# Moving the statistics of the third token tile behind the second tile's k projection

## The chip, the cores and the metric

The kernel runs on all 8 cores of one Trainium2 chip (two dies, cores 0 to 3 and 4 to 7). The same program runs on every core, with other data; the cores exchange nothing. The time is the device time of the slowest core, in microseconds (us).

## What is computed

A layer norm of x (4 x 4096 x 1024), then an attention-like branch and a feed-forward branch with ternary weights, both added to x:

```python
xn = _layernorm(x)
# attention branch
qkv = einsum('btd,de->bte', xn, Wqkv) + bqkv
q, k, v = split(qkv, 3)
q = q / norm(q);  k = k / norm(k)
kv = sum(k * v, axis=-2, keepdims=True)      # over all 4096 tokens of a batch
attn = einsum('btd,de->bte', q * kv, Wout) + bout
# feed-forward branch (tlin = matmul with ternary w, scaled by s)
h = silu(tlin(xn, w1)) * tlin(xn, w2)
h = gelu(tlin(h, h1));  h = gelu(tlin(h, h2))
out = x + attn + tlin(h, w3)
```

The sum kv runs over all tokens of a batch entry. Each core writes 2048 tokens, but computes k and v for all 4096 tokens of its batch entry.

## The kernel before

The data lie feature-major: 128 features on the partitions, tokens along the free axis. Tokens are taken in tiles of TT = 1024. Tiles g = 0 to 3 cover all 4096 tokens for k and v; tiles 4 and 5 are tiles 0 and 1 again, now for q and the feed-forward branch. The big buffer Gb has three regions for normalised tiles; tiles 0, 1 and 2 lie in regions 0, 1 and 2 (REGION), tile 3 in region 0 again.

A small scheduler (class Sched) records each operation with its engine and the tokens it waits for, and emits them engine by engine in the order in which they were recorded. So the order of the Python calls is the order in each engine's queue. SP's queue issues x loads, POOL's (GpSimd) weight loads, and PE, DVE and ACT have one queue each. S.emit() ends a block of the program; there are two blocks, and the engines meet between them.

The pieces that matter:

- plan_stats(g) (L202): for each of 8 feature chunks an x load of 512 KB into one of two slots xs (L185), a cast to bf16 on DVE (L210), a Square on ACT (L214), and four matmuls with a matrix of ones, which sum x into PSUM tile PA and x squared into PB. Then a tail on DVE and ACT (L237 to L251) makes the reciprocal deviation rstd_b and u_b. Then the 8 chunks of x are loaded a second time and normalised into Gb with two DVE operations each (L259 and L261). These eight are called xn(g) below.
- plan_proj: 4 weight units (512 KB each, ring of 5 slots) of two output chunks each. An output chunk is 16 matmuls of 128x512, which need all 8 normalised chunks, into one of the PSUM tiles PC, PD, PB in turn. An evacuation on ACT frees the PSUM tile: L393 for k, L312 for q, L416 for v. For k and q a Square (L398, L317) and two matmuls with ones into PA follow for each chunk.
- plan_norm_rstd (L297, L301): Ln and Exp on ACT of the norm in PA, written to rstdn_b. The Ln waits for the last norm matmul and, by extra=[st["kv_prev_dve"]], for the plan_kv before it, which still reads rstdn_b.
- plan_kv: for 8 chunks two large DVE operations (L366, L369) and a tiny addition to kv_acc (L373). Below it is kv(0) for t = 0 and kv(1) for t = 1.

All of it that matters here is the first block. Its order is: stats(0) with xn(0); for t = 0: k projection of tile 0, its norm, stats(1) with xn(1), v projection of tile 0, stats(2) with xn(2), kv(0); for t = 1: k projection of tile 1, its norm, q projection of tile 4, v projection of tile 1, kv(1). In the prediction k(0), v(0), k(1), q and v(1) are these projections. The second block begins with stats(3) and the first feed-forward projections; tile 2 is read only after them, in the segment loop that makes k and v of tiles 2 and 3.

Of the kernel before, what the change touches and what calls it, by code (L numbers as in the profile page):

```python
# [106 lines left out]
def build_program(stop=None):  # L107
# [16 lines left out]
    with ExitStack() as _ctx:  # L124
# [26 lines left out]
        PA = en(nc.psum_tensor("PA", [128, TT], F32))  # L151
        PB = en(nc.psum_tensor("PB", [128, TT], F32))
# [36 lines left out]
        def dma_w(unit_ap):  # L189
            j, slot, ftok = w_ring.next()  # L190
            tok = S.op("gpsimd", lambda e, o=slot, i=unit_ap: e.dma_start(out=o[:, :], in_=i),  # L191
                       waits=[ftok], inc=w_ring.semn[j])
            return j, slot, tok

        def mm(ps_name, hs, lhsT, rhs, start, stop, waits=(), inc=None):
            return S.op("tensor",
                        lambda e, p=PS[ps_name], h=hs, l=lhsT, r=rhs, a=start, b=stop:
                        e.matmul(p[:, h * 512:(h + 1) * 512], l, r, start=a, stop=b),  # L198
                        waits=waits, inc=inc)
# [72 lines left out]
        def plan_proj(units, g, evac, ping=("PC", "PD", "PB"), pre=None):  # L272
            xn_toks = xn_toks_g[g]
            k = 0
            for iu, (unit_ap, ocs) in enumerate(units):
                jw, wslot, tw = pre[iu] if pre is not None else dma_w(unit_ap)
                last_tok = None
                for jo, oc in enumerate(ocs):
                    ps = ping[k % len(ping)]
                    k += 1  # L280
                    t_mm = None
                    for kc in range(DC):
                        for hh in range(2):
                            t_mm = mm(ps, hh,
                                      wslot[:, kc * 256 + jo * 128: kc * 256 + (jo + 1) * 128],
                                      xn_sl(g, kc, hh),
                                      start=(kc == 0), stop=(kc == DC - 1),
                                      waits=[tw, psum_free[ps], xn_toks[kc]],
                                      inc="s_pe" if (kc == DC - 1 and hh == 1) else None)
                    last_tok = t_mm  # L290
                    psum_free[ps] = evac(oc, ps, t_mm)
                w_ring.set_free(jw, last_tok)

        def plan_norm_rstd(norm_ps, norm_last, dst=None, extra=()):
            if dst is None:
                dst = rstdn_b
            t_ln = S.op("scalar", lambda e, p=norm_ps, d=dst: e.activation(  # L297
                d[:, :], PS[p][:, :], AF.Ln),
                waits=[norm_last] + list(extra), inc="s_ac")
            psum_free[norm_ps] = t_ln  # L300
            t_rk = S.op("scalar", lambda e, d=dst: e.activation(  # L301
                d[:, :], d[:, :], AF.Exp, scale=f32(-0.5)),
                waits=[t_ln], inc="s_ac")
            return t_rk
# [53 lines left out]
        with (  # L358
            nc.sbuf_tensor("kB2", [128, DC * TT], BF16) as kB2,
            nc.sbuf_tensor("vA", [128, DC * TT], BF16) as vA,  # L360
            nc.sbuf_tensor("vB", [128, DC * TT], BF16) as vB,
            nc.sbuf_tensor("prod", [128, TT], F32) as prod,
        ):
            def plan_kv(kbuf, vbuf, t_rk, kev, vev):
                for oc in range(DC):
                    tp = S.op("vector", lambda e, o=oc, kb=kbuf, vb=vbuf: e.tensor_mul(  # L366
                        prod[:, :], kb[:, o * TT:(o + 1) * TT], vb[:, o * TT:(o + 1) * TT]),
                        waits=[kev[oc], vev[oc]], inc="s_dv")
                    tm = S.op("vector", lambda e, o=oc: e.scalar_tensor_tensor(  # L369
                        prod[:, :], prod[:, :], 1.0, rstdn_b[:, :], ALU.mult, ALU.mult,  # L370
                        accum_out=kvp[:, o:o + 1]),
                        waits=[tp, t_rk], inc="s_dv")
                    st["kv_done"] = S.op("vector", lambda e, o=oc: e.tensor_add(  # L373
                        kv_acc[:, o:o + 1], kv_acc[:, o:o + 1], kvp[:, o:o + 1]),
                        waits=[tm], inc="s_dv")
                st["kv_prev_dve"] = st["kv_done"]
                if kbuf is qkvt:
                    st["kv_dve_par0"] = st["kv_done"]

            plan_stats(0, "PA", "PB")  # L380
            xn_toks_g[4] = xn_toks_g[0]
            for t in range(NT1):
                kbuf = qkvt if t % 2 == 0 else kB2
                vbuf = vA if t % 2 == 0 else vB
                kev, vev = {}, {}
                norm_last = [None]

                pend_n = []

                def k_evac(oc, ps, t_mm, _kb=kbuf, _kev=kev, _nl=norm_last):  # L390
                    if len(pend_n) >= 2:
                        pend_n.pop(0)()
                    tk = S.op("scalar", lambda e, o=oc, p=ps: e.activation(  # L393
                        _kb[:, o * TT:(o + 1) * TT], PS[p][:, :], AF.Identity,
                        bias=cst[:, 8 + o:9 + o]),
                        waits=[t_mm], inc="s_ac")
                    jq, qslot, fq = sq_ring.next()
                    tq = S.op("scalar", lambda e, o=oc, q=qslot: e.activation(  # L398
                        q[:, :], _kb[:, o * TT:(o + 1) * TT], AF.Square),
                        waits=[tk, fq], inc="s_ac")  # L400

                    def nmm(oc_=oc, jq_=jq, qslot_=qslot, tq_=tq):
                        t_n = None
                        for hh in range(2):
                            t_n = mm("PA", hh, ones_sb[:, :], qslot_[:, hh * 512:(hh + 1) * 512],
                                     start=(oc_ == 0), stop=(oc_ == DC - 1),
                                     waits=[tq_, psum_free["PA"]],
                                     inc="s_pe" if hh == 1 else None)
                        sq_ring.set_free(jq_, t_n)
                        _nl[0] = t_n  # L410
                    pend_n.append(nmm)
                    _kev[oc] = tk
                    return tk

                def v_evac(oc, ps, t_mm, _vb=vbuf, _vev=vev):
                    tv = S.op("scalar", lambda e, o=oc, p=ps: e.activation(  # L416
                        _vb[:, o * TT:(o + 1) * TT], PS[p][:, :], AF.Identity,
                        bias=cst[:, 16 + o:17 + o]),
                        waits=[t_mm], inc="s_ac")
                    _vev[oc] = tv  # L420
                    return tv

                plan_proj([(wqkv[4 + i, :, :], [2 * i, 2 * i + 1]) for i in range(4)],
                          t, k_evac, pre=st.get("pre_k"))
                while pend_n:
                    pend_n.pop(0)()
                t_rk = plan_norm_rstd("PA", norm_last[0],
                                      extra=[st["kv_prev_dve"]])
                if t == 0:
                    plan_stats(1, "PA", "PB")  # L430
                if t == NT1 - 1:
                    plan_qproj(4)
                plan_proj([(wqkv[8 + i, :, :], [2 * i, 2 * i + 1]) for i in range(4)],
                          t, v_evac)
                war[t % 3] = S.pe_tok()
                st["pre_k"] = ([dma_w(wqkv[4 + i, :, :], ) for i in range(4)]
                               if t + 1 < NT1 else None)
                if t == NT1 - 1:
                    st["pre_ffn"] = [dma_w(w1[0, :, :]), dma_w(w2[0, :, :])]
                if t == 0:  # L440
                    plan_stats(2, "PA", "PB")
                plan_kv(kbuf, vbuf, t_rk, kev, vev)

            if stop == "p1":
                S.op("sync", None, waits=[st["kv_done"]])
            S.emit()
# [336 lines left out]
```

How the kernel before makes its waits and increments, by code:

```python
            def body(eng):  # L69
                for _, fn, waits, tok in items:
                    for wt in waits:
                        sname, val = wt[0], wt[1]
                        key = (ename, sname)
                        if self.done.get(key, 0) >= val:
                            continue
                        eng.wait_ge(self.sems[sname], val)
                        self.done[key] = val
                    if fn is not None:
                        inst = fn(eng)
                        if tok is not None:
                            inst.then_inc(self.sems[tok[0]],
                                          16 if tok[0] in self.DMA_SEMS else 1)
```

## Time and profile before

| | us |
|---|---|
| median of the 2 runs shown | 3077.19 |
| lowest, highest | 3072.51, 3081.87 |
| profiled execution, device time | 3087.21 |
| its span (slowest core, core 2) | 3085.7 |
| PE busy in the span | 2882.0 (93%) |
| DVE busy, ACT busy | 378.6 (12%), 464.6 (15%) |

The profile is one execution; times are us from the start of a core's span unless marked ns. A row of the timeline gives the start, the length, the engine, the line, the operation with what it writes and reads and its shape, the count of instructions merged, and in brackets how long the engine was idle before it and what ended that. Lengths of merged matmul groups are modelled and may overlap the next group by a fraction of a us; the distance between starts is the safer measure.

### The profile page before, as it was taken

How to read it: one execution, taken by the hardware profiler on the slowest of the kernel's cores; microseconds unless marked ns; L12 is line 12 of the kernel's file. 1: busy time of each engine (PE TensorE's matmuls, PEld its weight loads, DVE VectorE, ACT ScalarE, POOL GpSimd, SP SyncE). 2: the span in 40 equal slices, each digit the busy share in tenths (PEclk: the TensorE clock that was granted, in tenths of full speed). 3: DMA queues.
4: the chain of work that ended last, by engine and by line, in shares of the span. 5: the costliest groups of instructions: out<-in, count | busy, mean ns of one | idle time of the engine just before them, and what ended most of it. 6: DMA issues, size and time to landing. Idle time of an engine off the chain costs nothing.

```text
span 3085.7 us, 30706 instructions; the slowest of 8 cores (3046.7 to 3085.7 us)
## 1 busy us (share of the span) xinstructions
PE 2882.0 (93%) x13056; PEld 1283.0 (42%) x13056; DVE 378.6 (12%) x440; ACT 464.6 (15%) x463; POOL 219.9 (7%) x420
## 2 busy tenths in 40 slices
PE   3876799899999999999988899999999999999987
PEld 0322244344444444444433344444444444444433
DVE  3254211443000000000011221100000000000011
ACT  1433211351000000000020031100000000000100
POOL 0000000010000000000000000000000000000000
PEclk8888799999999999999999999999999999999998
DMA  6561544785444444444445654444444444444453
GB/s 162 126 159 32 116 80 72 156 137 96 76 77 78 78 75 76 75 78 78 77 102 116 130 97 75 82 74 77 75 75 76 77 78 78 75 75 76 75 107 92
DMA packets 76598, 278.93 MB, mean 90 GB/s; under 512 B 8752, under 2 KB 8880, under 8 KB 76464
## 3 DMA queue, kind: packets, MB, share of 16 engines
q0 software_dynamic: 59904, 218.13, 42.6%
q1 hardware_dynamic: 16560, 58.85, 6.4%
q8 instruction: 105, 1.72, 0.2%
q14 instruction: 29, 0.24, 0.0%
HBM read 486.66 MB, written 8.39 MB: 160 GB/s over the span
## 4 chain that ended last, share of the span: by engine, by line
PE 82%; DMA 5%; DVE 2%; ACT 1%; issue 0%; SPq 0%; DVEq 0%; ACTq 0%
PE PD L198 23%; PE PC L198 23%; PE PB L198 18%; PE PA L198 18%; DMA xs<-x_fm 3%; DMA out_fm<-os 1%; DVE os L701 1%; DVE os L695 0%; ACT os L667 0%; DVE xb L210 0%; DVE tmp_f L259 0%; ACT Ab L626 0%; DVE Ab L498 0%; DVE Gb L261 0%; DVE rstd_b L242 0%
## 5 line engine op out<-in xcount | busy, mean ns | idle before, releaser
L198 PE MATMUL PC<-Gb,wr 128*128 128x512 bf16 x2080 | 479.0, 383 | 23.1 <-DVE Gb L261 23.1
L198 PE MATMUL PD<-Gb,wr 128*128 128x512 bf16 x2080 | 474.3, 381 | 0.0
L198 PE MATMUL PB<-Gb,wr 128*128 128x512 bf16 x1728 | 393.0, 381 | 4.1 <-DVE rstd_b L242 4.1
L198 PE MATMUL PD<-Ab,wr 128*128 128x512 bf16 x1536 | 359.1, 388 | 39.3 <-ACT os L667 39.3
L198 PE MATMUL PC<-Ab,wr 128*128 128x512 bf16 x1536 | 347.2, 379 | 1.6 <-ACT os L667 1.6
L198 PE MATMUL PA<-Gb,wr 128*128 128x512 bf16 x1536 | 347.2, 379 | 0.0
L198 PEld LDWEIGHTS PC<-Gb,wr 128*128 128x128 bf16 x2080 | 204.4, 99 | 277.1 <-issue 36.9
L198 PEld LDWEIGHTS PD<-Gb,wr 128*128 128x128 bf16 x2080 | 204.3, 98 | 247.6 <-issue 4.3
L198 PEld LDWEIGHTS PB<-Gb,wr 128*128 128x128 bf16 x1728 | 169.5, 98 | 210.6 <-issue 8.3
L191 POOL DMA_DIRECT2D wr<-h_t x256 | 135.1, 528 | 1616.6 <-PE PB L198 798.4
L198 PEld LDWEIGHTS PD<-Ab,wr 128*128 128x128 bf16 x1536 | 152.9, 100 | 230.8 <-issue 58.0
L198 PE MATMUL PA<-Ab,wr 128*128 128x512 bf16 x1024 | 231.4, 379 | 2.9 <-DVE Ab L498 1.7
L198 PE MATMUL PB<-Ab,wr 128*128 128x512 bf16 x1024 | 231.5, 379 | 0.0
L198 PEld LDWEIGHTS PC<-Ab,wr 128*128 128x128 bf16 x1536 | 150.4, 98 | 182.8 <-issue 2.0
L198 PEld LDWEIGHTS PA<-Gb,wr 128*128 128x128 bf16 x1536 | 150.2, 98 | 181.4
L198 PEld LDWEIGHTS PA<-Ab,wr 128*128 128x128 bf16 x1024 | 99.9, 98 | 124.4 <-issue 3.8
L198 PEld LDWEIGHTS PB<-Ab,wr 128*128 128x128 bf16 x1024 | 100.0, 98 | 121.0
L210 DVE CAST xb<-xs 128x1024 bf16<-128x1024 f32 x40 | 27.8, 694 | 989.5 <-ACT sq L214 895.3
L695 DVE SCALAR_TENSOR_TENSOR os<-PC,cst,os 128x1024 f32<-128x1024 f32 x8 | 10.3, 1284 | 1083.6 <-PE PC L198 1083.6
L198 PE MATMUL PA<-xb,ones_sb 128*128 128x512 bf16 x80 | 37.9, 577 | 81.5 <-DVE xb L210 80.1
L191 POOL DMA_DIRECT2D wr<-w_t x96 | 50.7, 528 | 716.5 <-PE PD L198 577.8
L626 ACT ACTIVATE Ab<-PC,cst 128x1024 bf16<-128x1024 f32 x16 | 17.8, 1113 | 405.2 <-PE PD L198 405.2
(83 smaller groups left out, 1005.1 us busy)
## 6 DMA issues: line engine op xcount, KB each, us to landing
wr<-h_t POOLq DMA_DIRECT2D x256, 512.0 KB, 5.6
xs<-x_fm SPq DMA_DIRECT2D x96, 512.0 KB, 4.8
wr<-w_t POOLq DMA_DIRECT2D x96, 512.0 KB, 5.4
wr<-wqkv_t POOLq DMA_DIRECT2D x56, 512.0 KB, 5.8
out_fm<-os SPq DMA_DIRECT2D x16, 512.0 KB, 3.4
wr<-wout_t POOLq DMA_DIRECT2D x8, 512.0 KB, 6.4
cst<-consts SPq DMA_DIRECT2D x1, 64.0 KB, 1.9
ones_sb<-ones_bf SPq DMA_DIRECT2D x1, 32.0 KB, 2.6
```

What stands on the lines that cost most here:

```text
L191: tok = S.op("gpsimd", lambda e, o=slot, i=unit_ap: e.dma_start(out=o[:, :], in_=i), waits=[ftok], inc=w_ring.semn[j])
L198: e.matmul(p[:, h * 512:(h + 1) * 512], l, r, start=a, stop=b),
L210: tb = S.op("vector", lambda e, o=bslot, i=xslot: e.tensor_copy(o[:, :], i[:, :]), waits=[tx, fb], inc="s_dv")
L626: t_g = S.op("scalar", lambda e, o=oc, p=ps: e.activation(dst[:, o * TT:(o + 1) * TT], PS[p][:, :], AF.Gelu, scale=s_cst[:, s_col0 + o:s_c ...
L695: t2o = S.op("vector", lambda e, p=ps, o=oslot, c=oc: e.scalar_tensor_tensor(o[:, :], PS[p][:, :], cst2[:, 32 + c:33 + c], o[:, :], ALU.mu ...
L701: t3o = S.op("vector", lambda e, o=oslot, x_=xslot: e.tensor_add(o[:, :], o[:, :], x_[:, :]), waits=[t2o, tx], inc="s_dv")
```

## The change

The call plan_stats(2, "PA", "PB") is taken out of the turn t = 0, where it stood between the v projection of tile 0 and plan_kv, and is put into the turn t = 1, between the norm of the k projection of tile 1 and the q projection. Nothing else is changed; every operation is still there.

```diff
@@ -428,6 +428,8 @@
                                       extra=[st["kv_prev_dve"]])
                 if t == 0:
                     plan_stats(1, "PA", "PB")
+                else:
+                    plan_stats(2, "PA", "PB")
                 if t == NT1 - 1:
                     plan_qproj(4)
                 plan_proj([(wqkv[8 + i, :, :], [2 * i, 2 * i + 1]) for i in range(4)],
@@ -437,8 +439,6 @@
                                if t + 1 < NT1 else None)
                 if t == NT1 - 1:
                     st["pre_ffn"] = [dma_w(w1[0, :, :]), dma_w(w2[0, :, :])]
-                if t == 0:
-                    plan_stats(2, "PA", "PB")
                 plan_kv(kbuf, vbuf, t_rk, kev, vev)
```

## Rows read from the trace of the kernel before

**Rows 1.** The cores: span of each and its granted TensorE clock.

```profile
core 2: 3085.7 us, clock 0.965
...
core 7: 3046.7 us, clock 0.974
```

**Rows 2.** Chain that ended last, core 2: start, length, what; its first long pieces.

```profile
307.60 3.87 DMA xs<-x_fm
...
312.40 10.90 DMA xs<-x_fm
```

**Rows 3.** Timeline of PE on core 2, 74 to 276 us.

```profile
74.46 4.71 PE L198 MATMUL PD<-Gb,wr 128*128 128x512 bf16 x16
...
104.67 0.59 PE L198 MATMUL PA<-sq,ones_sb 128*128 128x512 bf16 x2 [1.75 <-ACT sq L398]
106.58 1.10 PE L198 MATMUL PA<-xb,ones_sb 128*128 128x512 bf16 x4 [1.32 <-ACT rstdn_b L297]
...
126.65 4.23 PE L198 MATMUL PC<-Gb,wr 128*128 128x512 bf16 x16
...
151.44 3.62 PE L198 MATMUL PD<-Gb,wr 128*128 128x512 bf16 x16
165.35 1.01 PE L198 MATMUL PA<-xb,ones_sb 128*128 128x512 bf16 x2 [10.30 <-DVE xb L210]
...
186.78 4.88 PE L198 MATMUL PC<-Gb,wr 128*128 128x512 bf16 x16
191.50 3.62 PE L198 MATMUL PD<-Gb,wr 128*128 128x512 bf16 x16
...
221.04 3.62 PE L198 MATMUL PC<-Gb,wr 128*128 128x512 bf16 x16
...
251.03 1.01 PE L198 MATMUL PA<-sq,ones_sb 128*128 128x512 bf16 x2 [19.47 <-ACT sq L317]
...
275.20 3.62 PE L198 MATMUL PC<-Gb,wr 128*128 128x512 bf16 x16
```

**Rows 4.** Timeline of DVE on core 2, 72 to 308 us.

```profile
72.28 1.23 DVE L261 TENSOR_TENSOR Gb<-tmp_f,u_b 128x1024 bf16<-128x1024 f32 x1
...
108.90 0.69 DVE L210 CAST xb<-xs 128x1024 bf16<-128x1024 f32 x1 [31.80 <-ACT sq L214]
...
162.45 1.23 DVE L261 TENSOR_TENSOR Gb<-tmp_f,u_b 128x1024 bf16<-128x1024 f32 x1
...
222.87 1.22 DVE L366 TENSOR_TENSOR prod<-qkvt,vA 128x1024 f32<-128x1024 bf16 x1
...
246.05 0.16 DVE L373 TENSOR_TENSOR kv_acc<-kv_acc,kvp 128x1 f32<-128x1 f32 x1
...
307.09 0.16 DVE L373 TENSOR_TENSOR kv_acc<-kv_acc,kvp 128x1 f32<-128x1 f32 x1
```

**Rows 5.** Timeline of ACT on core 2, at 246 us.

```profile
246.36 1.02 ACT L297 ACTIVATE rstdn_b<-PA 128x1024 f32<-128x1024 f32 x1 [25.90 <-DVE kv_acc L373]
```

**Rows 6.** DMA issues on core 2, 100 to 350 us: count, size, median us to landing.

```profile
xs<-x_fm SPq DMA_DIRECT2D x38, 512.0 KB, 4.6
```

**Rows 7.** Timeline of POOL on core 2, one weight load.

```profile
102.60 0.53 POOL L191 DMA_DIRECT2D wr<-wqkv_t  x1 [7.24 <-PE PA L198]
```

**Rows 8.** The same timelines on core 5: DVE's last normalised pieces, PE's projection starts.

```profile
73.07 1.23 DVE L261 TENSOR_TENSOR Gb<-tmp_f,u_b 128x1024 bf16<-128x1024 f32 x1
...
126.26 4.41 PE L198 MATMUL PC<-Gb,wr 128*128 128x512 bf16 x16
...
160.58 1.23 DVE L261 TENSOR_TENSOR Gb<-tmp_f,u_b 128x1024 bf16<-128x1024 f32 x1
...
185.95 5.28 PE L198 MATMUL PC<-Gb,wr 128*128 128x512 bf16 x16
...
220.60 3.62 PE L198 MATMUL PC<-Gb,wr 128*128 128x512 bf16 x16
...
278.72 3.62 PE L198 MATMUL PC<-Gb,wr 128*128 128x512 bf16 x16
```

## The prediction

> **What bounds the kernel now.** I began with the cores: the metric is the slowest core, and its execution here spans 3085.7 us where the quickest core needs 3046.7 [rows 1]. TensorE executes everything that counts (the page shows it busy for 93% of the span), so the change can only bring what it takes out of TensorE's idle time, or puts in. Next comes the chain of waits. Its last-ended chain starts at 307.60 us, at the first x load of the second block of the program [rows 2]. The two blocks meet in a barrier: nothing of the second block, its x loads and weights included, is issued before the last DVE instruction of the first, the kv_acc addition that starts at 307.09 [rows 4]. So the first block is one sum from 0 to 307.25 us, and whatever it loses or gains shifts the remaining 2778 us as a whole. The change lies wholly in this block.
>
> Then the instructions of TensorE in order of time [rows 3]. The reader is to see six pieces there: the k projection of the first token tile (from 74.46 on, its first chunk before that), its statistics neighbour stats(1) (106.58 to 126.65), v of the first tile (126.65 to 155.06), an idle stretch of 10.30 us, stats(2) (165.35 to 186.78), k of the second tile (186.78 to 221.04), q, and v of the second tile (from 275.20). In q there is a second hole: 19.47 us of idle before 251.03. Its releaser is not the one that is really late. ScalarE's Ln of the k norm started only at 246.36, after 25.90 us of waiting for kv_acc [rows 5]. It must not overwrite rstdn_b before kv(0) has read it. And kv(0) ran on DVE from 222.87 to 246.21, 23.3 us, because DVE's queue held all of stats(2) and its eight normalisations ahead of it [rows 4], though its inputs had been complete since shortly after 155 us. ScalarE's queue holds the q evacuations behind that Ln, so TensorE ran out of PSUM after three output chunks.
>
> **The change, part by part.** No instruction is added or removed; stats(2) moves, in every queue, from before kv(0) and k(1) to behind the k(1) norm.
>
> SP's queue holds x loads alone: stats(1), its eight normalisation loads, stats(2), its eight. Their order does not change. POOL's weight loads keep their order too. What changes is when slots come free.
>
> 1. *kv(0) first on DVE.* The last piece of xn(1) is started at 162.45 and takes 1.23. kv(0) then follows at once and ends at 163.7 + 23.3 = 187.0 instead of 246.2. The Ln of k(1) then waits only for its own norm.
>
> 2. *k(1) directly after v(0).* TensorE stands idle after 155.06 anyway; now it works the first chunk of k(1) in that time, for as many input pieces as DVE has normalised, and ends that chunk behind the last piece. The same has already happened once in this trace, at the start: k(0) follows xn(0) piece by piece, then the norm, the Ln, stats(1), then the next projection. From the start of the last normalised piece (72.28) to the start of that next projection (126.65) it takes 54.37 us [rows 3, 4]. With the same chain the q projection starts at 162.45 + 54.37 = 216.82.
> This contains the two costs that the new order adds: 1.32 us in which stats waits for the Ln to free PA, and stats held up by its loads. I take the whole term from that row.
>
> 3. *Is kv(0) hidden?* By the same row k(1)'s norm would end at 162.45 + (104.67 - 72.28) = 194.8; kv(0) is done at 187.0. That leaves 7.8 us of cover. Without the cover the Ln, stats(2)'s first matmul and then q would be late by what is missing. The casts of stats(2) stand behind kv(0), so the first two start at 187.0, where today the first is through before 165.35. Their release of the x slots is what lets loads three and four go: at about 188 plus 4.6 us to land [rows 6], 193, while the third cast cannot go before TensorE has read the first (about 196.7). In stats(1) too, the cast at 108.90 had waited 31.80 us with its data there, so I expect the same pace. In both places a last weight load is under way just before (POOL issues one at 102.60 [rows 7]).
>
> 4. *q after stats(2).* It meets the same queue as k(1) does today: the tail of stats on ScalarE, then an evacuation and a Square for each chunk. k(1) took 221.04 - 186.78 = 34.26 us. q then ends, and v(1) starts, at 216.82 + 34.26 = 251.08, against 275.20 today: **24.1 us less**.
>
> 5. *The other work that moved.* xn(2) now runs on DVE during q: eight loads and sixteen operations. Today the stats tail and xn(2) are through when kv(0) starts, 222.87 - 186.78 = 36.1 us after stats(2) ends; moved, that is 216.8 + 36.1 = 252.9. kv(1) can start when the first chunk of v(1) is computed and evacuated, some 4 us after 251.08, at 255. Were this cover of 2 us gone, kv(1) would still have slack: it takes 23.3 us of DVE, spread today over v(1), whose chunks follow each other at (151.44 - 126.65) / 7 = 3.54 us, 28.3 in all. I count nothing here. The region that xn(2) writes is read only in the segment loop of the second block. v(1), its evacuations, kv(1) and the barrier follow v(1) at today's distance: 307.25 - 275.20 = 32.05. The barrier moves to 283.1.
>
> The clock: a projection after a stall starts slowly, at the lower of the two levels of the granted clock (1.2 against 2.4 GHz). k(1) began with a group that took 4.88 us where the next took 3.62 [rows 3]. TensorE had waited for pieces before the second group of k(0), and my term of 54.37 holds that loss. With a warm start instead (the second group of k(0), at 74.46, took 4.71, that of k(1), at 191.50, took 3.62) 1.1 us more is saved. The Trainium skill (TensorE: Matmul & The Clock Gate, section on what is actually happening) has the array at 1.2 GHz after idling and at 2.4 GHz after sustained work. By it the two short waits left inside k(1)'s first chunk could cost that 1.1 us or not. The trace agrees on the two levels, and the sum would be 24.1 or 25.2.
>
> How typical is core 2? Core 5 by its own rows [rows 8]: q would start at 160.58 + (126.26 - 73.07) = 213.77, v(1) at 213.77 + (220.60 - 185.95) = 248.42, against 278.72: 30.3 us less. Core 2, which sets the metric here, is one end, core 5 the other. I take **26 us**, nearer to core 2. The profiled execution took 3087.2 (span 3085.7), which becomes 3061. It was a slow one of its kind: the median is 3077.2, of runs from 3072.5 to 3081.9. The same 26 us off the median gives 3051.
>
> **The rivals.**
>
> *A. Only part of it arrives.* stats(2) at its new place, or the first chunk of k(1), takes some 10 us more than the row I copied; two x loads in flight beside weight loads can take 10.90 us for one [rows 2]. For it: these loads start later, in another phase against the weights. Against: the place is built like stats(1). Gain about 14: 3063.
>
> *B. It is given back after the barrier.* The cores' spans differ by 39 us [rows 1], more than the gain, though TensorE's work is the same on all. If the slowest core is made by collisions of loads later on, the shift may leave it where it is: 3077. Against: the shift is nearly rigid on each core.
>
> *C. Slower than before.* The six x loads of stats(2) that are issued after kv(0) come one by one at the 10.90 us of [rows 2], 65 us, where stats(1) needed 17.75 from its third cast (108.90) to its end: 48 more, 24 gained, so 3101. It decides above (17.75 + 24.1) / 6 = 7.0 us for each load. Against it stands the median landing of 4.6 [rows 6], and two in flight. The Trainium skill (DMA: Bandwidth & Descriptors, section Issuing engines are not separate DMA queues) says that transfers of all issuing engines run on the same 16 DMA engines and interleave. That speaks for C wherever weights are due; here the 10.90 us load agrees, and it fell where the program issued weights at the same moment.
>
> *D. More than 61 us.* The two holes together are 29.8 us on core 2, and no step above reaches further; only an unforeseen better phase of the later loads would do it.
>
> **How the numbers follow.** Forecast (24 to 30 saved, carried to the end) 0.75, A 0.12, B 0.07, C 0.04, D 0.02. The forecast with its own spread of gain (30.3 from the lowest run 3072.5 is 3042; 24.1 from the highest 3081.9 is 3058) gives 3042 to 3058. Widened for A and for the scatter of the runs: 3038 to 3067. This measurement can hardly tell less than 2% (61.5 us) from no change, and the forecast is 0.8%: faster by over 2% 0.03 (D and a little more), within 2% 0.95, slower by over 2% 0.02 (the worse half of C).
>
> **What would show it.** The Ln of the second k norm waits for TensorE and not for kv_acc, and the hole in q is gone. kv(0) starts at about 164. k(1)'s first chunk lies in 155 to 165; stats(2) ends near 217; v(1) starts near 251; the barrier falls near 283; from there on the profile is that of before, shifted. I am wrong if stats(2)'s casts wait for DMA by more than a few us each, if kv(1) waits for xn(2), or if the stretch behind the barrier grows.

## The result and the profile after

The changed kernel takes 3053.7 us in the median of all its 13 executions, the kernel before beside it 3088.0 in the median of 10; the ratio to before is 0.9888, with a 95% interval from 0.9865 to 0.9912. From the level of 3088 us that is 34.5 us less (27 to 42). It is less than the 2% that this measurement is asked to tell, but clear of its scatter.

In some executions of both kernels the cores of one die show a lower granted clock than the others, as cores 4 to 7 do in the profiled execution of the changed kernel, so the ratios and the means below leave such dies and executions out. The rows below are of core 2. The cores, with span and granted clock:

```profile
core 2: 3046.9 us, clock 0.974
...
core 5: 3151.0 us, clock 0.941
```

First TensorE in order of time on core 2 (the same columns as in [rows 3]):

```profile
152.88 2.75 PE L198 MATMUL PC<-Gb,wr 128*128 128x512 bf16 x12
157.37 0.59 PE L198 MATMUL PC<-Gb,wr 128*128 128x512 bf16 x2 [1.73 <-DVE Gb L261]
162.26 1.01 PE L198 MATMUL PC<-Gb,wr 128*128 128x512 bf16 x2 [4.30 <-DVE Gb L261]
163.07 5.36 PE L198 MATMUL PD<-Gb,wr 128*128 128x512 bf16 x16
...
193.92 0.59 PE L198 MATMUL PA<-sq,ones_sb 128*128 128x512 bf16 x2 [1.75 <-ACT sq L398]
195.89 1.02 PE L198 MATMUL PA<-xb,ones_sb 128*128 128x512 bf16 x4 [1.38 <-ACT rstdn_b L297]
...
214.18 3.71 PE L198 MATMUL PC<-Gb,wr 128*128 128x512 bf16 x16
...
247.27 3.62 PE L198 MATMUL PC<-Gb,wr 128*128 128x512 bf16 x16
```

The first chunk of k(1) now stands where TensorE had 10.30 us of idle after v(0): twelve of its matmuls run at 152.88, straight after v(0), two at 157.37, the last two at 162.26 as soon as DVE has delivered the last piece. 6.03 us of idle are left between them (1.73 and 4.30). The 19.47 us hole of [rows 3] has no counterpart. q begins at 214.18 and v(1) at 247.27, against 221.04 and 275.20.

Then DVE on core 2:

```profile
160.89 1.23 DVE L261 TENSOR_TENSOR Gb<-tmp_f,u_b 128x1024 bf16<-128x1024 f32 x1
162.22 1.23 DVE L366 TENSOR_TENSOR prod<-qkvt,vA 128x1024 f32<-128x1024 bf16 x1
...
185.69 0.16 DVE L373 TENSOR_TENSOR kv_acc<-kv_acc,kvp 128x1 f32<-128x1 f32 x1
185.96 1.49 DVE L210 CAST xb<-xs 128x1024 bf16<-128x1024 f32 x2
198.21 0.69 DVE L210 CAST xb<-xs 128x1024 bf16<-128x1024 f32 x1 [10.76 <-ACT sq L214]
...
248.12 1.23 DVE L261 TENSOR_TENSOR Gb<-tmp_f,u_b 128x1024 bf16<-128x1024 f32 x1
252.33 1.23 DVE L366 TENSOR_TENSOR prod<-kB,vB 128x1024 f32<-128x1024 bf16 x1 [2.98 <-ACT vB L416]
...
279.17 0.16 DVE L373 TENSOR_TENSOR kv_acc<-kv_acc,kvp 128x1 f32<-128x1 f32 x1
```

kv(0) starts right behind the last piece of xn(1) and ends at 185.85. The first two casts of stats(2) follow at once. The third waits 10.76 us for a slot of xb, and the last to read that slot is ScalarE's first Square of stats(2), at 196.98 in the ACT rows below, behind the Ln and Exp of k(1)'s norm. xn(2) ends at 249.35, and kv(1) waits 2.98 us for its first input: xn(2) is hidden beside q. The block ends at 279.33 instead of 307.25.

ScalarE's Ln, which waited 25.90 us for kv_acc in [rows 5], now waits for its own norm:

```profile
194.72 1.02 ACT L297 ACTIVATE rstdn_b<-PA 128x1024 f32<-128x1024 f32 x1 [0.94 <-PE PA L198]
195.83 1.06 ACT L301 ACTIVATE rstdn_b<-rstdn_b 128x1024 f32<-128x1024 f32 x1
196.98 4.50 ACT L214 ACTIVATE sq<-xb 128x1024 bf16<-128x1024 bf16 x4
```

The busy time of each engine from the end of v(0) to the start of v(1), core 2 (bounds: length, then PE, weight loads, DVE, ACT, POOL busy, then granted clock, DMA share, GB/s), of the changed kernel:

```profile
152.88:247.27 94.39, 75.78 (x321) 31.45 (x320) 53.95 (x63) 49.54 (x46) 4.76 (x9) 0.93 0.60 144
```

and of the kernel before:

```profile
155.06:275.20 120.14, 80.16 (x321) 32.28 (x322) 54.68 (x63) 49.53 (x46) 4.75 (x9) 0.79 0.47 114
```

25.8 us of length are gone; the other 2.2 of the 27.9 by which v(1) starts sooner lie in v(0), which ended sooner in this execution. Idle time of TensorE fell from 40.0 to 18.6 us, and its busy time by 4.4, with the same matmuls at a mean granted clock of 0.93 instead of 0.79: the holes had cost their own length and, behind them, slower matmuls.

Behind the block everything is only shifted. The chain that ended last, from the barrier on, core 2 of the changed kernel:

```profile
280.10 4.52 DMA xs<-x_fm
285.55 12.70 DMA xs<-x_fm
...
316.88 5.23 PE PB L198 x16
```

It is the chain of [rows 2]: x loads, one of them long (12.70, before 10.90). From the last kv_acc addition to the first feed-forward matmul it is 37.7 us in both kernels on core 2.

### The profile page after: what moved, and what is told of

Its sections match the earlier page's. It is cut to its first block, busy times and chain, and to the rows that moved or that the text cites. A ratio compares the mean times of both kernels' runs of the same rounds, so it can differ in the third digit from the quotient of the medians.

```text
span 3151.3 us, 30463 instructions; the slowest of 8 cores (3016.9 to 3151.3 us)
## 1 busy us (share of the span) xinstructions
PE 2966.6 (94%) x12795; PEld 1307.2 (41%) x13056; DVE 378.7 (12%) x440; ACT 464.5 (15%) x463; POOL 219.9 (7%) x420
## 4 chain that ended last, share of the span: by engine, by line
PE 85%; DMA 4%; DVE 1%; issue 1%; ACT 1%; DVEq 0%; SPq 0%; ACTq 0%
PE PD L198 24%; PE PC L198 24%; PE PB L198 19%; PE PA L198 19%; DMA xs<-x_fm 3%; DMA out_fm<-os 1%; DVE os L701 0%; DVE xb L210 0%; DVE tmp_f L259 0%; DVE os L695 0%; ACT os L667 0%; ACT Ab L626 0%; ACT sq L214 0%; DVE Ab L498 0%; DVE Gb L261 0%
## 5 line engine op out<-in xcount | busy, mean ns | idle before, releaser
L198 PE MATMUL PC<-Gb,wr 128*128 128x512 bf16 x2039 | 496.0, 395 | 33.0 <-DVE Gb L261 30.6
L198 PE MATMUL PD<-Gb,wr 128*128 128x512 bf16 x2044 | 494.0, 394 | 2.9 <-DMA wr<-wqkv_t 0.4
L198 PE MATMUL PB<-Gb,wr 128*128 128x512 bf16 x1687 | 409.6, 395 | 6.4 <-DVE rstd_b L242 4.1
L198 PE MATMUL PA<-Gb,wr 128*128 128x512 bf16 x1507 | 366.6, 396 | 2.0
L198 PE MATMUL PC<-Ab,wr 128*128 128x512 bf16 x1507 | 357.5, 389 | 3.7 <-ACT os L667 1.7
L198 PEld LDWEIGHTS PA<-Ab,wr 128*128 128x128 bf16 x1024 | 100.8, 99 | 126.0 <-issue 12.1
```

## The experiments

Two measures are used. The first is *D*, from the start of the last piece of xn(1) on DVE to the start of v(1) on TensorE, averaged over the profiled cores. It leaves out when xn(1) happened to arrive, which differs by up to 16 us between cores and runs. The second is the ratio. Where the slowest core is too coarse, the mean span of the cores over all executions is given with its standard error; it is compared only with the runs of before on the same chip.

| kernel | xn(1) | D | v(1) | barrier | first feed-forward | ratio |
|---|---|---|---|---|---|---|
| before | 162.8 | 113.9 | 276.6 | 308.5 | 346.5 | 1 |
| changed | 162.3 | 86.5 | 248.9 | 280.8 | 318.7 | 0.9888 |
| changed, again | 163.2 | 85.7 | 248.9 | 280.8 | 318.5 | 0.9882 |
| e1 kv(0) first | 164.6 | 112.9 | 277.5 | 309.4 | 347.5 | 0.9977 |
| e2 freed buffers | 161.8 | 91.6 | 253.4 | 285.3 | 322.4 | 0.9942 |
| e3 changed, freed | 164.3 | 86.2 | 250.5 | 282.4 | 319.5 | 0.9908 |
| e4 kv(0) late | 165.2 | 87.6 | 252.8 | 302.5 | 340.7 | 0.9973 |
| e5 stats(2) after q | 164.2 | 85.8 | 250.0 | 305.1 | 342.3 | - |
| e6 stats(3) in v(1) | 167.3 | 86.6 | 253.9 | 295.5 | 297.8 | 0.9841 |
| e7 kv(0) longer | 167.0 | 101.4 | 268.4 | 300.3 | 338.5 | - |

(us from the start of the span, means over 4 cores of the profiled execution for the changed kernel, its repetition, e3 and e7, and over 8 for the others; "xn(1)" and "barrier" are the starts of the last xn(1) piece and of the last kv_acc addition, the others are starts too. e5 and e7 have no usable ratio.)

### The changed kernel once more

> The changed kernel once more, beside the others of this group. Theory (what the first block saves is all): barrier and first feed-forward matmul 26 to 29 us earlier than before, ratio 0.991. Rival (the phase of the later loads gains or loses something as well): the part behind the barrier is shorter or longer than before by more than 5 us in the median over the cores; the ratio of 0.9888 measured first would need some 6 us there.

The ratio is 0.9882 (0.9849 to 0.9915), and the barrier comes at 280.8, 27.7 us earlier. The mean span fell from 3062.1 (standard error 1.1) to 3030.0 (2.1) on this chip, by 32.1 with an error of 2.4. e3, whose first block has the same length, fell by 28.8 with an error of 1.6. Both agree with 27.7 within two errors. Behind the barrier the cores of this profile need 2751.7 us in the median, those of before 2750.4, so the rival's 5 us are not seen in it; in the first profile of the changed kernel it was 2762.1, over four cores that lie 30 us apart, too coarse to tell either way. The runs show no part of the gain that comes from behind the barrier. The slowest core of eight varies more than that: 34.5 us is the first block's 27.7 plus something that these runs do not tell from chance.

### e1: kv(0) ahead, stats(2) where it was

```diff
-                if t == 0:
-                    plan_stats(2, "PA", "PB")
                 plan_kv(kbuf, vbuf, t_rk, kev, vev)
+                if t == 0:
+                    plan_stats(2, "PA", "PB")
```

> The kernel before with only kv(0) recorded ahead of stats(2); stats(2) stays between v(0) and k(1). Theory (the move pays because kv(0)'s 23.3 us on DVE find a place beside k(1)): the 19.5 us hole in q goes, but stats(2)'s casts start at about 187 instead of 164, so the idle stretch after v(0) grows from 10.3 to about 32 us; v(1) starts near 275, ratio 1.000. Rival (the late kv(0) is the whole cause, any place ahead will do): v(1) starts near 254, ratio 0.993.

The ratio is 0.9977 (0.9950 to 1.0004); mean span 3061.8 (1.7) against 3062.1 (1.1). TensorE on core 2:

```profile
191.54 1.87 PE L198 MATMUL PA<-xb,ones_sb 128*128 128x512 bf16 x4 [35.84 <-DVE xb L210]
...
212.51 4.06 PE L198 MATMUL PC<-Gb,wr 128*128 128x512 bf16 x16
```

The hole in q is gone, and one of 35.84 us stands after v(0) where 10.30 stood. v(1) starts at 277.5, before at 276.6. An early kv(0) alone is worth nothing, because it then delays the casts that TensorE waits for; the rival would have had v(1) at 254.

### e2: nothing waits for kv(0), order as before

k of tile 0 goes to the quarter of Gb that the first block does not use; the reciprocal norm of tile 1 goes to os1. Both are needed: q's evacuation (L312) writes into qkvt, where k of tile 0 lies, and by its own wait (kv_dve_par0, L315) stands behind kv(0) as the Ln does.

```diff
-                kbuf = qkvt if t % 2 == 0 else kB2
+                kbuf = Gb[:, 3 * DC * TT:4 * DC * TT] if t % 2 == 0 else kB2
...
-                t_rk = plan_norm_rstd("PA", norm_last[0],
-                                      extra=[st["kv_prev_dve"]])
+                rn = rstdn_b if t == 0 else os1
+                t_rk = plan_norm_rstd("PA", norm_last[0], dst=rn)
```

> The kernel before with its order unchanged, but nothing waits for kv(0): k of tile 0 goes into the unused upper quarter of Gb instead of qkvt, and the reciprocal norm of tile 1 into os1 instead of rstdn_b. Theory: the hole of 19.5 us in q goes and the cold start behind it (about 1.3 us); the idle 10.3 us after v(0) stays; v(1) starts near 254.5, 20.8 us earlier, ratio 0.993. Rival (kv(0) on DVE meanwhile delays something else): less than 15 us earlier.

The ratio is 0.9942 (0.9917 to 0.9968), the mean span 21.2 us less (error 1.9). D falls by 22.3, expected 20.8. TensorE on core 2:

```profile
169.12 1.01 PE L198 MATMUL PA<-xb,ones_sb 128*128 128x512 bf16 x2 [12.58 <-DVE xb L210]
...
256.52 0.59 PE L198 MATMUL PA<-sq,ones_sb 128*128 128x512 bf16 x2 [1.75 <-ACT sq L317]
```

The idle stretch after v(0) is still there; in q only the usual 1.75 us before the last norm pair is left. So the waits for kv(0) were worth 22 of the changed kernel's 27 us, shown by removing their cause in place. The other 5 I put down to the first chunk of k(1), worked in the idle stretch, less the new wait for the Ln; no run takes them apart.

### e3: the changed kernel with the same buffers freed

> The changed kernel with the same two buffers freed. Theory (kv(0) is covered by 7.8 us in the changed kernel): no difference to the changed kernel, barrier within 1.5 us of its, ratio 0.991. Rival (the Ln or stats(2) is still held up by kv(0)): up to 5 us better than the changed kernel.

D is 86.2, against 86.5 and 85.7 of the changed kernel, and the ratio 0.9908 (0.9883 to 0.9933). Freeing the buffers brings nothing more: kv(0) is covered where the change put it.

### e4: k(1) first, kv(0) behind xn(2)

```diff
                 else:
                     plan_stats(2, "PA", "PB")
+                    plan_kv(*kv0_args)
...
-                plan_kv(kbuf, vbuf, t_rk, kev, vev, rn)
+                if t == 0:
+                    kv0_args = (kbuf, vbuf, t_rk, kev, vev, rn)
+                else:
+                    plan_kv(kbuf, vbuf, t_rk, kev, vev, rn)
```

> The changed kernel with the two freed buffers, and kv(0) recorded behind stats(2) and xn(2) in place of ahead of them. Nothing waits for kv(0) here, so this keeps the k(1) part of the move and gives up the early kv(0). Theory (DVE's order sets the end of the first block once both reductions stand behind xn(2)): v(1) starts where it does in the changed kernel, near 248, but DVE does kv(0) from about 249 to 273 and kv(1) until about 296, so the barrier falls near 296, 16 us later than in the changed kernel; ratio 0.996. Rival (only TensorE's holes count): barrier near 280, ratio 0.990.

The edit shown is against e3, whose freed buffers this run has too. TensorE is nearly as good as there (D 87.6 against 86.2), but the barrier falls at 302.5, and the ratio is 0.9973 (0.9947 to 0.9999). The mean span is 7.8 us (error 2.2) less than that of before on its chip, the barrier 6.0 us earlier: the time follows the barrier and not TensorE's holes. DVE on core 2:

```profile
254.31 1.23 DVE L261 TENSOR_TENSOR Gb<-tmp_f,u_b 128x1024 bf16<-128x1024 f32 x1
255.64 1.23 DVE L366 TENSOR_TENSOR prod<-Gb,vA 128x1024 f32<-128x1024 bf16 x1
...
279.11 1.23 DVE L366 TENSOR_TENSOR prod<-kB,vB 128x1024 f32<-128x1024 bf16 x1
...
302.31 0.16 DVE L373 TENSOR_TENSOR kv_acc<-kv_acc,kvp 128x1 f32<-128x1 f32 x1
```

Both reductions, 23.5 us each, stand behind xn(2) and end the block alone. I had expected 296. The two reductions were sized right; xn(2) ended 6.2 us later than I took from the changed kernel (255.54 and 249.35 on core 2). 1.4 us of that are a later xn(1); the rest lies in stats(2), xn(2) and their loads.

### e5: stats(2) one place further back

```diff
-                else:
-                    plan_stats(2, "PA", "PB")
                 if t == NT1 - 1:
                     plan_qproj(4)
+                    t_rq0 = plan_q_rstd()
+                    plan_stats(2, "PA", "PB")
```

> The changed kernel with stats(2) one place further back, between q and v(1); the Ln and Exp of the q norm move in front of it. Theory (xn(2) needs q as its cover): v(1) starts near 248 as in the changed kernel, but xn(2) runs to about 284 beside v(1) and kv(1) behind it until about 308, so the barrier is back at 308 and the ratio at 1.000. Rival (the place behind k(1) is as good as any later one): barrier near 280, ratio 0.990.

v(1) starts with nearly the same D (85.8), but the barrier comes at 305.1, expected 308. Only two executions can be used, of 3070.3 and 3092.5; that is too little for a ratio, and only the profile is read. On core 1, DVE and then TensorE:

```profile
280.99 1.23 DVE L261 TENSOR_TENSOR Gb<-tmp_f,u_b 128x1024 bf16<-128x1024 f32 x1
282.32 1.23 DVE L366 TENSOR_TENSOR prod<-kB,vB 128x1024 f32<-128x1024 bf16 x1
...
305.51 0.16 DVE L373 TENSOR_TENSOR kv_acc<-kv_acc,kvp 128x1 f32<-128x1 f32 x1
```

```profile
310.72 1.01 PE L198 MATMUL PA<-xb,ones_sb 128*128 128x512 bf16 x2 [33.27 <-DVE xb L210]
```

xn(2) has lost q as its cover, kv(1) starts 33 us after v(1) does, and TensorE stands idle for 33.27 us before stats(3). All but some 3 us of the gain at the barrier is given back by DVE. The place matters on both sides: behind k(1), but with q still to come.

### e7: how much cover kv(0) has

Each product of kv(0) is computed three times.

```diff
                 for oc in range(DC):
+                    if kbuf is qkvt:
+                        for _r in range(2):
+                            S.op("vector", lambda e, o=oc, kb=kbuf, vb=vbuf: e.tensor_mul(
+                                prod[:, :], kb[:, o * TT:(o + 1) * TT], vb[:, o * TT:(o + 1) * TT]),
+                                waits=[kev[oc], vev[oc]], inc="s_dv")
```

> The changed kernel with kv(0) made longer by 16 more products of 1.33 us each, 21.3 us (each product is computed three times). Theory (the Ln of k(1)'s norm and stats(2)'s casts have about 8.9 us of cover): v(1) starts 12 to 17 us later than in the changed kernel (21.3 less the cover, and up to 5 for x loads three and four, which then land late). Rival (the cover is larger, kv(0) does not matter where it now stands): under 5 us later.

D grows to 101.4, by 14.8 over the first run of the changed kernel. No ratio is given; the profile is read. On core 5:

```profile
196.91 0.59 PE L198 MATMUL PA<-sq,ones_sb 128*128 128x512 bf16 x2 [1.75 <-ACT sq L403]
210.94 1.86 PE L198 MATMUL PA<-xb,ones_sb 128*128 128x512 bf16 x4 [13.44 <-ACT rstdn_b L297]
```

TensorE's wait for the Ln grew from 1.38 (core 2 of the changed kernel) to 13.44, so 12.1 of the 21.3 added (16 products at 1.33) came through, and the cover was about 9; from the trace of the changed kernel it is 194.72 - 185.85 = 8.9, the start of the Ln less the end of kv(0). The other 3 us lie in stats(2) and its neighbours; I did not take them apart.

### e6: stats(3) spread over v(1)

One large wait is left in the neighbourhood of the first block, the 38 us behind the barrier. stats(3) is cut into its eight chunks and each is recorded behind one chunk of v(1):

```diff
+                    t_rq0 = plan_q_rstd()
+                    s3_step, s3_finish = plan_stats(3, "PA", "PB", defer_xn=True, steps=True)
+
+                    def v_hook(i, _a=(kbuf, vbuf, t_rk, kev, vev)):
+                        s3_step(i)
+                        if i >= 1:
+                            plan_kv(*_a, ocs=[i - 1])
+                    plan_proj([(wqkv[8 + i, :, :], [2 * i, 2 * i + 1]) for i in range(4)],
+                              t, v_evac, ping=("PC", "PD"), hook=v_hook)
...
-                emit_xn3 = plan_stats(3, "PA", "PB", defer_xn=True) if t == 0 else None
+                emit_xn3 = s3_finish() if t == 0 else None
```

> The changed kernel with the sums of stats(3) taken out of the second block and spread over v(1): one of its eight chunks (load, cast, Square, four matmuls) behind each of v(1)'s chunks, kv(1) piece by piece between them, v(1) on two PSUM tiles; the second block begins its first chunk on PC. Theory (behind the barrier TensorE waits 36 to 38 us for x loads that could have been made before it): v(1) grows by 8 x 0.86 us to 34.5, the barrier falls near 286, the first feed-forward matmul near 288 in place of 317 (core 2 of the changed kernel); 28 us less than the changed kernel, ratio to before 0.981. Rival (casts queued behind xn(2) and kv pieces hold TensorE up, or x loads collide with weights): half of it or less, ratio 0.986 or more.

The ratio is 0.9841 (0.9822 to 0.9859); the mean span is 51.6 us (error 2.2) less than that of before on its chip. It beats both kernels. TensorE on core 2:

```profile
260.59 0.59 PE L198 MATMUL PA<-xb,ones_sb 128*128 128x512 bf16 x2 [4.06 <-DVE xb L211]
261.02 5.30 PE L198 MATMUL PD<-Gb,wr 128*128 128x512 bf16 x16
...
296.53 1.86 PE L198 MATMUL PB<-sq,ones_sb 128*128 128x512 bf16 x4 [3.88 <-PEq L85]
298.19 4.22 PE L198 MATMUL PC<-Gb,wr 128*128 128x512 bf16 x16
```

From the last piece of xn(1) to the first feed-forward matmul it is 130.6 us, in the changed kernel 156.4: 25.8 less, expected 28. What is missing fits the first cast of stats(3), which waits for its x load behind xn(2) (4.06 us of idle on core 2, then a slow group of 5.30); no run removes it. The expected absolute times (288) missed by 10: 5 us because xn(1) itself came later in this run, the rest because v(1) was longer by more than the eight added pieces.

## Why the prediction was right, point by point

1. *The first block shifts the rest as a whole.* Right: from kv_acc to the first feed-forward matmul 37.7 us before and after on core 2, 38.0 and 37.9 in the mean. Rival B (given back later) is refuted by the interval, which lies below 1, and by the mean spans of the changed kernel's repetition and of e3.

2. *kv(0) first, from 163.7 to 187.0.* It ran from 162.22 to 185.85 (23.6 us), behind an xn(1) that came 1.6 us earlier. The prediction named one thing that waits for kv(0), the Ln. q's evacuations wait for it too, as e2 tells; the move frees both, so the sum does not change.

3. *k(1), its norm, the Ln and stats(2) as in the copy at the start of the trace: 54.37 us.* Measured 214.18 - 160.89 = 53.29. Two errors inside cancel in part. k(1) to its last norm pair took 33.03, not 32.39: it started even slower than the row I copied (5.36 for the second group, 4.71 there), so the warm start that I held possible did not come. The rows tell why: after 1.73 us of idle the pair took 0.59 at a granted clock of 1.00 (2.4 GHz), after 4.30 it took 1.01 at 0.50 (1.2 GHz), and the second group ran at 0.66 in the mean. The windows of the changed kernel:

```profile
157.37:157.96 0.59, 0.59 (x2) 0.10 (x2) 0.00 (x0) 0.00 (x0) 0.00 (x0) 1.00 0.90 208
162.26:163.07 0.81, 0.81 (x2) 0.26 (x3) 0.81 (x1) 0.00 (x0) 0.00 (x0) 0.50 0.69 56
163.07:168.26 5.19, 5.19 (x17) 2.00 (x16) 4.38 (x8) 2.17 (x2) 0.00 (x0) 0.66 0.27 99
```

The Trainium skill (TensorE: Matmul & The Clock Gate, What's actually happening) has the array at half clock after idling. The trace agrees: 0.50 behind the 4.30 us of idle. And from that norm pair to q it was 20.26 instead of 21.98: two of the casts that waited for their x loads came 0.6 and 1.3 us sooner after the ones before them than in stats(1). The third cast came as in the copied row, but its wait ends with ScalarE's Square (ACT sq in both traces) and not with TensorE's first read, as the prediction had it.

4. *q after stats(2): 34.26.* Measured 33.09. q started warm (a group of 3.71) where k(1) of [rows 3] started with 4.88.

5. *Sum: D of 88.63 predicted for core 2; measured 86.4 there and 86.5 in the mean.* As the gain at the barrier: 24.1 predicted on core 2, 27.9 measured, 27.7 in the mean over cores. The value of 26 that I took between cores 2 and 5 was low by 1.7. Of the 3.8 us between 24.1 and 27.9, 1.6 are the earlier xn(1) of this execution, which no term held. The other 2.2 are terms of the sum: stats(2)'s pace (1.7) and q's cold start (1.2), less k(1)'s slower start (0.6).

6. *The cover of kv(0), 7.8 us.* Measured 8.9 in the trace and 9 by e7. *xn(2) covered by q with 2 us to spare*: measured 2.98 (the wait of kv(1) in the rows above), and e5 shows what happens without: the barrier 24 us later than in the changed kernel.

7. *The time.* 3051 forecast, 3053.7 measured. That closeness is luck in good part, two errors that cancel. I subtracted 26 from a median of two runs, 3077.2. With ten runs the median of before was 3088.0, so the base was 10.8 us low; and the measured gain, 34.5, is 8.5 more than 26 and has an interval that leaves 26 just outside. The step that failed is the last: the level of before rested on two executions. The mechanism and its price in the first block held (26 against 27.7); where the rest of the 34.5 comes from stays open, and may be scatter.

Rival A (only part arrives) did not occur: stats(2) at its new place was quicker than its model. Rival C needed more than 7.0 us for each of the six loads behind kv(0); the six took from 198.21, the third cast, to 214.18, 2.7 us each. Rival D (over 61 us) is outside the interval. Long loads there were, 12.70 us in the chain behind the barrier, with three weight loads under way that GpSimd had issued at 280.11; before it was 10.90, so they cost both kernels alike. That the weights make them long is not shown: no run moved them.

## What to carry to other kernels

A hole on TensorE is named in the profile by the last link (ACT sq), but its cause can sit two queues away: here a reduction on VectorE that stood behind work nobody needed yet. When moving a block of work in an in-order schedule, check three things in the trace: what the move uncovers in front (e1), what must still follow it to hide its tail (e5), and how much cover each hidden piece has in us (e7). If the same pattern of stages already occurs elsewhere in the trace, its length from mark to mark is a price that holds the waits inside it too; a sum over instructions was not tried here. For k(1) with stats(2) it held here to 1.1 us, in which two errors of 0.6 and 1.7 us cancel in part.

## What the runs showed that I had not expected

The busy time of TensorE between the end of v(0) and the start of v(1) fell by 4.4 us although its matmuls stayed the same (windows above: granted clock 0.79 and 0.93). Of the 25.8 us saved there on core 2, 21.4 were idle time and 4.4 came from the higher clock, 0.2 us for each us of idle time removed.

The arrival of xn(1) varies from 157.5 to 173.7 us between cores and runs, and barrier times with it. On a single core that is more than most of the effects studied here, so two kernels are compared from a common mark or in the mean over cores. And with the same barrier time, spans of cores still differ by 30 us (core 1 needs 2738 us behind the barrier in the changed kernel, core 2 needs 2768). I did not look for the cause.
